# Filling the expert slots in small pieces between the feature copies of a fused convolution and expert kernel

## What is computed

```python
x = x + _L0_conv_ref(_ln_c(x), ...)    # gating, 3x3 attention from sigmoids, a fixed smoothing, down_w, instance norm
t = _to_tokens(x)
t = t + _L0_ffn_ref(_ln_t(t), Wg, W1, W2, W3, b3)   # 8 experts, top 2, act = silu(h) * g
x = _from_tokens(t, x)
x = x + _L1_conv_ref(_ln_c(x), codebook, bias)      # depthwise 7x7, taps hashed from a codebook
t = _to_tokens(x)
t = t + _L1_ffn_ref(_ln_t(t), gate_w, w1, b1, w2, b2)  # 8 experts, top 2, capacity 1.25
x = _from_tokens(t, x)
```

```python
logits = jnp.einsum('bcyx,bcyxk->byxk', sig, sigp) / c
attn = jax.nn.softmax(logits, axis=-1)
g2 = jnp.einsum('byxk,bcyxk->byxc', attn, ffp)
out_csa = g2.reshape(b, c, h, w)            # a reshape that mixes pixels and channels
cat = jnp.concatenate([gus_out, out_csa], axis=1)
z = jnp.einsum('oi,biyx->boyx', down_w, cat)
```

## Time and profile before

| | us |
|---|---|
| median of 3 runs | 2296.94 |
| lowest and highest | 2284.54, 2297.9 |
| profiled execution | 2298.95 |
| its span | 2297.2 |

### The profile page before, as it was taken

One profiled execution on the slowest core, in us unless ns is written; L12 is line 12 of the kernel. 1 busy time (PEld: TensorE's weight loads), 2 busy tenths in 40 slices (PEclk: granted clock), 3 DMA queues, 4 the chain that ended last, 5 costly groups with the idle time before them and its releaser, 6 DMA issues.

```text
span 2297.2 us, 35957 instructions
## 1 busy us (share of the span) xinstructions
PE 1782.5 (78%) x10285; PEld 1501.1 (65%) x10285; DVE 1200.4 (52%) x4533; ACT 773.0 (34%) x1691; POOL 895.6 (39%) x939
## 2 busy tenths in 40 slices
PE   4898888988687878888899993883787777777833
PEld 3788777876576777777688883883675455444522
DVE  4477677575445333565567875569871111111156
ACT  1333332332333333444455542011673222222311
POOL 2000003554555666565554452000026666666510
PEclk9999999999899999999999996997888889899855
DMA  3266654557555654555556545642001222122167
GB/s 113 65 112 123 109 98 109 113 113 157 135 134 142 164 145 133 168 152 168 161 155 194 182 145 137 130 122 115 1 14 45 54 55 56 54 54 57 40 226 223
DMA packets 263909, 268.41 MB, mean 117 GB/s; under 512 B 69460, under 2 KB 232079, under 8 KB 262588
## 3 DMA queue, kind: packets, MB, share of 16 engines
q1 hardware_dynamic: 201532, 198.41, 34.4%
q0 software_dynamic: 28416, 55.89, 8.2%
q10 hardware_dynamic: 33792, 12.06, 2.0%
HBM read 167.37 MB, written 89.67 MB: 112 GB/s over the span
## 4 chain that ended last, share of the span: by engine, by line
PE 26%; another core or an unknown queue 23%; DVE 17%; ACT 9%; issue 9%; DMA 9%; POOL 3%; DVEq 2%; SPq 2%; POOLq 0%; ACTq 0%
PE zp L756 4%; PE tp L898 4%; ACT arena L1301 3%; DMA out<-arena 3%; DMA slots<-arena 3%; POOL slots L635 2%; DVE arena L1697 2%; PE tp L908 2%; DVE arena L1871 2%; PE gp L920 2%; PE zp L920 1%; ACT arena L1202 1%; ACT arena L1217 1%; PE tp L836 1%
## 5 line engine op out<-in xcount | busy, mean ns | idle before, releaser
L635 POOL DMA_INDIRECT slots<-arena x256 | 254.6, 995 | 504.7 <-issue 425.2
L674 POOL DMA_INDIRECT results<-arena x304 | 303.5, 998 | 295.7 <-DVE arena L1682 213.8
L706 POOL DMA_INDIRECT arena<-table,arena x160 | 153.2, 958 | 350.4 <-DVE arena L1859 301.9
L898 PE MATMUL tp<-arena 128*128 128x256 f32 x912 | 232.6, 392 | 48.3 <-ACT arena L1209 44.7
L756 PE MATMUL zp<-arena 128*128 128x256 f32 x1024 | 238.2, 387 | 10.3 <-ACT arena L1115 10.0
L1884 DVE TENSOR_TENSOR arena<-zp,arena 128x512 f32<-128x512 f32 x40 | 27.7, 692 | 396.9 <-remote 361.1
L756 PEld LDWEIGHTS zp<-arena 128*128 128x128 f32 x1024 | 195.3, 194 | 38.1 <-ACT arena L1115 11.7
L1697 DVE SCALAR_TENSOR_TENSOR arena<-tp,arena 128x256 f32<-128x256 f32 x304 | 135.7, 480 | 151.0 <-PE tp L908 52.1
L898 PEld LDWEIGHTS tp<-arena 128*128 128x128 f32 x912 | 165.8, 195 | 72.9 <-ACT arena L1209 51.4
L1202 ACT ACTIVATE arena<-tp 128x512 f32<-128x512 f32 x152 | 90.9, 598 | 361.5 <-remote 227.6
L720 POOL DMA_INDIRECT results<-arena x160 | 156.5, 978 | 129.2 <-DVE arena L1884 89.8
(11 more groups left out here) (290 smaller groups left out, 3186.3 us busy)
## 6 DMA issues: line engine op xcount, KB each, us to landing
arena<-in_L_ffn_W SPq DMA_DIRECT2D x304, 192.0 KB
arena<-results SPq DMA_DIRECT2D x56, 512.0 KB, 4.8
arena<-slots SPq DMA_DIRECT2D x152, 134.0 KB
arena<-taps SPq DMA_DIRECT2D x64, 224.0 KB, 4.6
table<-arena SPq DMA_DIRECT2D x4, 2144.0 KB
arena<-in_x SPq DMA_DIRECT2D x8, 1024.0 KB
arena<-arena SPq DMA_DIRECT2D x128, 64.0 KB
arena<-in_x SPq DMA_DIRECT2D x16, 512.0 KB
```

The lines of the kernel that those rows point to most:

```text
L635: g.indirect_dma_start(slots[r], bass.IndirectOffsetOnAxis(ap=slot[:, k, blk:blk + 1].bitcast(U32), axis=0), rows[:, blk, :], None, bounds ...
L674: g.indirect_dma_start(results, bass.IndirectOffsetOnAxis(ap=row_at[:, q:q + 1].bitcast(U32), axis=0), y_tiles[:, q, :], None, bounds_chec ...
L706: g.indirect_dma_start(quad_in[m][:, q, :], None, table, bass.IndirectOffsetOnAxis(ap=token_at[:, tile:tile + 1].bitcast(U32), axis=0)).th ...
L898: m = t.matmul(h_ps[c], w13[:, p, 0, P * c:P * c + P], tok_t[u], start=True, stop=True)
```

## The change

The seven fills are replaced by 32 of 7 rows each. Group 0 is filled in visits 1 and 2, group 1 in visits 3 and 4, eight pieces a visit, one behind every second feature copy. Visits 5 to 7 have no fill. SyncE waits for the fill row (`pool_const`) ahead of visit 0 instead of at the first fill, and GpSimd waits for 16 pieces of each group.

```diff
+FILLED, FILL_PARTS = {1: 0, 2: 0, 3: 1, 4: 1}, 16
+assert all(2 * G_PAIRS[g] % FILL_PARTS == 0 for g in range(2))
...
-            part = G_PAIRS[1] // 2
-            FILLS = {1: (0, 0, 40), 2: (0, 40, 36), 3: (0, 76, 2 * G_PAIRS[0] - 76),
-                     **{i: (1, part * (i - 4), part) for i in range(4, 8)}}
...
                             sp.dma_start(g2r[s][16 * k:16 * k + 16, b].rearrange("a j c -> a j c"), g2n[:, k, :]
                                          ).then_inc(sem("g2r_in"), 16)
-                if i in FILLS:
-                    if i == 1:
-                        sp.wait_ge(sem("pool_const"), 1)
-                    fill_slots(*FILLS[i])
-
+                            if i in FILLED and k % 2:
+                                rows_each = 2 * G_PAIRS[FILLED[i]] // FILL_PARTS
+                                part = FILL_PARTS // 2 * ((i - 1) % 2) + KB // 2 * b + k // 2
+                                fill_slots(FILLED[i], rows_each * part, rows_each)
+
+            sp.wait_ge(sem("pool_const"), 1)
             pipeline(sp, visit, aside=aside)
...
-            pool.wait_ge(sem("fill_out0"), 16 * 3)
+            pool.wait_ge(sem("fill_out0"), 16 * FILL_PARTS)
...
-            pool.wait_ge(sem("fill_out1"), 16 * 4)
+            pool.wait_ge(sem("fill_out1"), 16 * FILL_PARTS)
```

## The result

The changed kernel is slower: 2336.89 us median of 4 runs (2332.28 to 2338.4) against 2297.42 us (2284.54 to 2300.77), a ratio of 1.0171 with a 95% interval of 1.0148 to 1.0194. The profiled execution has a span of 2336.1 us, 38.9 more than before. Predicted were 2331 us. The ratios here and further down are the recorded ones; they differ from the quotient of the two medians by up to 0.15%.

What follows compares the result with a forecast made beforehand. Bound by TensorE's chain through the feature copies, then GpSimd's sends: profiled 2298.95 + 37.9 (hold) + 5.4 (slower products) - 9.4 (gain) = 2332.9 us, 2331 us as median; 8-in-10 range 2288 to 2354 us.

Steps and rivals of the forecast that it cites:

- The bound: The chain runs through TensorE and each visit's last feature copy in the front end, then through GpSimd's sends of group 0.
- The gain: At the expert stage's start, L887's wait of 7.85 us and 1.5 us of slower products go: 9.4 us saved.
- The hold: In visits 1 to 4 feature copies queue behind fill pieces, delaying TensorE: 37.9 us, plus 5.4 us of slower products.
- The first term: Delay of TensorE's L760 by late last copies: 7.5 us from visit 1, then 10.8, 8.7 and 10.9; together 37.9 us.
- VectorE's wait: The second image's L1514 waits for the first image's copies behind pieces: 3.0 us later in visit 1, DMA wait 2 to 5.
- What was said to cost nothing: SyncE's 25 more issues, 0.6 us each, are hidden (otherwise up to 2 us a visit); moved pool_const and GpSimd waits are met.
- (a): Rival: feature copies in the front end aren't held, so only the 9.4 us gain is left: 2287.5 us; chance 0.17.
- (b): Rival: the slowest DMA engine sets each front-end piece: hold 60 to 79 us, 2350 to 2366 us; chance 0.12.
- (c): Rival: GpSimd's long sends weren't the fills' doing, so the 9.4 us gain falls away: 2340 us; chance 0.06.

## Why the prediction was right

**The bound.** The chain through the feature copies in the front end and through the sends after it was read rightly. Taking the fills out of the sends' time ends the long bursts and L887's wait, and shifting the whole front end shifts the end.

**The gain: 9.4 us predicted, 7.6 seen from visit 7 on.** It was capped by TensorE's own front end as said. The 9.4 counted all of L887's 7.85 us, and 1.24 us of it stay, here as in the runs with the fills behind the copies. The sends take 165.4 us from the first to the last issued instead of 185.9, 20.6 us less for 30: beside copies, loads and taps seven bursts still wait 2.9 to 4.6 us, five of them over the 3 that I had named as the most. One reading of mine was off: the fill of visit 4 (329.12 us) went out before the first send, so the long bursts lay beside the fills and loads of visits 5 to 7, and the one of 13.42 us, which I put to visit 5, beside the fill of visit 6 (463.32 us). The sum doesn't change by it. With the hold taken away the gain is 12.9 us, on chip 4.

**The hold: 37.9 + 5.4 = 43.3 us predicted, 47.6 measured.** The first term is what L760 is late, counted from the visit's first copy. Predicted were 26.2 us for visit 1 and 28.9 for the others; it took 27.3, 29.5, 30.0 and 29.0 us, where it had been 18.6, 18.1, 20.2 and 18.0. That is 40.8 us for 37.9. The other 6.8 us, for 5.4, are products that take longer behind L760 and ahead of the next first copy. The rate fitted as well: from 200 to 226 us, in visit 2, the engines moved 208 GB/s on average, with no gap between the images, since the taps fill it. What I had wrong is inside the first term. TensorE waits twice a visit, 3.3 to 4.3 us at L852 and up to 8.3 at L760, and I counted one long wait; its clock falls at both, and 16.5 of the 47.6 us are the lower clock, where I named 5.4. Some 10 of them, the 16.5 less the 6.8 behind L760, lie inside the first term, which the bytes in the queue gave without them. Since part of the hold is sat out at L852, the wait at L760 itself is under the 9 to 13 us that I named for it.

**VectorE's wait.** The second image's L1514 moved from 9.66 us behind the visit's first copy to 13.53 us in visit 1, so by 3.9 us for 3.0. Its idle time is 7 us, since the 3.08 us for TensorE are now within it; I named 2 to 5.

**What was said to cost nothing.** The issues: right, by the runs with eight pieces and with one fill in the same place. Not foreseen was ScalarE: its eight tap issues take 10.9 to 13.0 us in the changed kernel instead of 5.7 to 7.0. There its next work on the images (L1108) is still released by VectorE in all three visits, 4.8, 2.3 and 1.1 us after ScalarE has issued its taps, so the issues aren't what is waited for; with the pieces together the taps' bytes and their issue made 21 of the 40 us.

**The rivals.** (a), copies not held, is ruled out by the L760 and L1514 waits. Its gain alone was seen when the place was changed. The prediction had no window with a fill over 254 GB/s; the one from 142 to 144 us of the kernel before shows 270, still under the 330 that (a) needs. (b), the slowest engine, asked for a hold of 60 us and more: 47.6. Its lower total is 2347.5 us by the terms given, and not 2350. (c), sends not slowed by fills: the fills gone, the burst beside the x loads of visit 5 (issued at 455.44 us) waits 2.90 us and the one beside the loads of 516.97 us 4.58, so loads alone don't make 10 us.

The Trainium skill ("DMA: Bandwidth & Descriptors", the section on queues, rings and completion order) has each DMA engine alternate between queue rows packet by packet. The runs here agree in part: SyncE's copies land ahead of a fill in ScalarE's queue, 9 us in visit 1, but take 7.85 us for 2.46; sends beside a fill get by less, and on chip 1 those beside the fill of visit 6 are landed at 481.1 us, when the fill is too (480.7). The figure of 436 GB/s under (a) is the one that the Trainium skill ("DMA: Bandwidth & Descriptors", the section on the anatomy of one DMA) fits to DMAs issued by GpSimd, and the fills are SyncE's; no run here reaches it.

## What to carry to other kernels

Cutting a background transfer into pieces doesn't make it harmless: what counts is how many bytes stand ahead of the transfer that somebody waits for next. Put it behind the last urgent one of the round, whole or in pieces, if the round's slack is long enough to drain it (here 3.84 MB in the 39 us until the next edge copies, 141.4 to 180.5 us). Another queue was no shelter: it made the loss larger here, 61.8 us for 37.4, by slower copies and by holding the engine that issues. And before crediting a stage with the time that a contended side chain loses, look at what else must be ready there: 21 to 28 us of sends were worth 8 to 13.

## What the runs showed of the hardware that I had not expected

- An engine's DMA issues take longer while transfers, also another engine's, are under way. ScalarE's eight tap issues took 5.7 to 7.0 us in the kernel before, 10.9 to 13.0 with SyncE's pieces between copies, 21 to 24 us beside four back-to-back pieces of SyncE, and 31 us behind a fill of 3.84 MB in its own queue. The instructions behind them on ScalarE wait as long.
- Pieces of 0.48 MB and the small copies between them moved at 197 to 253 GB/s together, and such pieces back to back, without copies, at 137 to 159 GB/s.
- With a fill of 3.84 MB in ScalarE's queue, copies in SyncE's passed it, but took 7.85 us from issue to landing instead of 2.46.
- The kernel before took 2297 us in one measurement and 2082 to 2090 us on three other occasions, and all of the difference lies behind the front end: in 440 us from 560 us on TensorE issued 2003 matmuls in one and 2541 on chip 1. The cause is open.
